# Second edge layer of a four-layer graph network: two of four message tiles weighed on ScalarE, scores copied from PSUM

## The chip, the cores and the metric

The kernel runs on one core of a Trainium2 chip. The metric is the device time of one launch in microseconds (us). It is a median of several runs; the kernel before has three. The profile is one execution of the same program. Its span runs from the first to the last recorded instruction.

## The reference

Four graph layers run one after the other over 50,000 nodes of 128 features and 25,000 edges, sorted by destination. Each adds its result to `x`. The change touches the second layer's edge pass:

```
h = max(layernorm(x), 0)
msgs = edge_weight[:, None] * h[src]
agg = segment_sum(msgs, dst)
x = x + agg @ W.T + b
```

The third layer is a graph attention layer. It needs, for every edge's destination, eight scores, and these are eight linear functions of the row `max(layernorm(x), 0)` after the second layer:

```
h = max(layernorm(x), 0)
(h @ W, a_src = h.att_src, a_dst = h.att_dst) -> 128 + 4 + 4 columns
```

## The kernel before, in words

All arithmetic is float32. The edges lie in 200 tiles of 125 edges, with one more row for what a segment carries over (126 rows, `RW`). Four tiles are a group (`GT` = 4), so that there are 50 groups (`NGE`). Each layer is a phase of its own, and the phases follow one another. The change lies in `phase_second`. Five engines run programs of their own there, tied by semaphores, as a software pipeline over steps `t`; at step `t` a group `g = t - k` is at stage `k`. One step therefore holds pieces of nine groups. On VectorE, ScalarE and SyncE the steps 12 to 43 stand in a loop of four steps a turn, the others are written out; TensorE's are all written out.

What is done for one group, with the line numbers of the profile:

- GpSimd issues four indirect DMAs (L526), which gather the 126 source rows of each tile into `second_xs`, four buffers. It may start on a group once ScalarE has finished the rows of the group four before (semaphore `rows`) and VectorE has copied its indices (L1240).
- VectorE subtracts a vector from `second_xs` (L1254), takes the statistics of each row (L1263, then L1294), and one step later 1/std and the bias (L1267, L1269). ScalarE takes the square root (L1324) between these.
- ScalarE normalises and applies Relu to each tile (L1314, `second_m<-second_xs`): four passes a group, each with a pointer for scale and one for bias.
- VectorE multiplies all four tiles `second_m` by the edge weights `k_wcol` in one instruction of 126x512 (L1258).
- TensorE turns the four tiles into `second_ps_agg` (L1365). VectorE runs a masked scan over them (L1306), which is the segment sum, into `second_at`. TensorE multiplies this by the layer's weights into `second_ps_y` (L1386), and VectorE adds it to the group's own rows `second_xp` (L1274). SyncE loads these rows (L1197) and stores them (L1216); it also loads the scan's mask (L1203).
- The statistics of the new rows are taken (L1284), ScalarE normalises them (L1314, `second_hr<-second_xp`), TensorE turns them (L1379), ScalarE copies the result to SBUF (L1348, `second_ht`), and TensorE makes `second_ps_g` of it, 136 columns a tile (L1395).
- ScalarE copies `second_ps_g` to SBUF as `second_g` (L1331) and signals `g_out`. SyncE stores `second_g` (L1210). VectorE copies the last eight columns of each tile from `second_g` to `l_SA` (L1290), with a pause on `g_out` before it, and signals `scores`, on which L1331 waits before it overwrites the buffer four groups later.

The order inside a step is written by hand, and the engines' queues are served in order. On VectorE it is L1240 (the indices of a later group), L1254, L1258, L1263 four times, L1267, L1269, L1274, two small copies (L1279, L1280), L1284 four times, L1290, L1294 eight times, L1306. On ScalarE it is L1324, L1331, four passes L1314 for `second_hr`, two for `second_m`, L1348, and the two other passes for `second_m`. On TensorE it is L1365, L1379, L1386, L1395. The statistics are awaited through the helper `gate`, which waits and then adds one to a semaphore that nobody reads:

```
def gate(kp, eng, sem, value):
    eng.wait_ge(sem, value)
    eng.sem_inc(kp.s_gate, 1)
```

## Time and profile before

| what | value |
|---|---|
| time, median of 3 runs | 3122.09 us |
| lowest and highest | 3106.39 and 3128.04 us |
| span of the profiled execution | 2606.6 us |
| second layer's edge pass, first gather to last score copy | 767.0 to 1092.1 us |
| VectorE (DVE) busy over the span | 78% |
| TensorE (PE) busy over the span | 73% |
| ScalarE (ACT) busy over the span | 66% |
| GpSimd (POOL) busy over the span | 50% |

The launch takes 515.5 us more than the span (3122.09 - 2606.6). The profiled execution has no separate time of its own beside its span here, so the two are set side by side: what lies around the span is taken as the same before and after. Shares over the whole span are a mean over the phases of four layers that have different limits; for a change in one phase the rows of that phase are to be read.

### The profile page before, as it was taken

How to read it: one execution, taken by the hardware profiler on the slowest of the kernel's cores; microseconds unless marked ns; L12 is line 12 of the kernel's file. 1: busy time of each engine (PE TensorE's matmuls, PEld its weight loads, DVE VectorE, ACT ScalarE, POOL GpSimd, SP SyncE). 2: the span in 40 equal slices, each digit the busy share in tenths (PEclk: the TensorE clock that was granted, in tenths of full speed). 3: DMA queues.
4: the chain of work that ended last, by engine and by line, in shares of the span. 5: the costliest groups of instructions: out<-in, count | busy, mean ns of one | idle time of the engine just before them, and what ended most of it. 6: DMA issues, size and time to landing. Idle time of an engine off the chain costs nothing. (4 is left out here: it accounts for less than half of the span.)

```text
span 2606.6 us, 48448 instructions
## 1 busy us (share of the span) xinstructions
PE 1899.9 (73%) x9715; PEld 1275.5 (49%) x9715; DVE 2027.9 (78%) x8016; ACT 1725.7 (66%) x4230; POOL 1311.4 (50%) x1309
## 2 busy tenths in 40 slices
PE   2445668888855666578884899566663999999996
PEld 1134445555534555468883444233332555555553
DVE  6855579999968999688885888588885777777773
ACT  3655679999965777589991444699994444444441
POOL 6755656666637666277760000000002677777773
PEclk9878889999986888889996999799997999999998
DMA  7989986666645777556662443699996544445540
GB/s 134 220 147 183 153 203 193 198 195 195 194 130 159 222 223 224 176 165 198 201 181 72 128 129 86 185 305 308 305 308 215 128 100 107 106 113 114 115 106 21
DMA packets 376244, 446.18 MB, mean 171 GB/s; under 512 B 103667, under 2 KB 225338, under 8 KB 376082
## 3 DMA queue, kind: packets, MB, share of 16 engines
q1 hardware_dynamic: 309970, 368.09, 50.8%
q0 software_dynamic: 59840, 74.08, 12.3%
q10 hardware_dynamic: 6272, 2.06, 0.5%
q8 instruction: 77, 1.26, 0.2%
q14 instruction: 85, 0.70, 0.1%
HBM read 288.86 MB, written 185.03 MB: 182 GB/s over the span
## 5 line engine op out<-in xcount | busy, mean ns | idle before, releaser
L2380 POOL DMA_INDIRECT mlp_bx<-t_X,k_bslot x2 | 2.0, 1012 | 611.7 <-POOLq L2647 611.4
L526 POOL DMA_INDIRECT second_xs<-t_XX,second_irs x200 | 205.4, 1027 | 115.8 <-issue 49.3
L2398 POOL DMA_INDIRECT out_dram<-mlp_ou,mlp_iro x200 | 212.6, 1063 | 83.2 <-issue 71.3
L2391 POOL DMA_INDIRECT mlp_xs<-t_X,mlp_irs x200 | 213.8, 1069 | 80.7 <-issue 55.7
L526 POOL DMA_INDIRECT project_xs<-t_XX,project_irs x200 | 199.6, 998 | 62.9 <-issue 58.3
L526 POOL DMA_INDIRECT a_xd<-in_x_dram,a_ird x152 | 152.6, 1004 | 129.1 <-DVE first_xo L968 84.9
L2439 DVE TENSOR_TENSOR_SCAN mlp_ms<-mlp_fm,mlp_ms,mlp_mm 128x500 f32<-128x500 f32 x98 | 123.4, 1260 | 120.2 <-ACT mlp_mm L2515 112.9
L2515 ACT ACTIVATE mlp_mm<-mlp_ps_m,mlp_bn 128x500 f32<-128x500 f32 x100 | 67.7, 677 | 187.1 <-PE mlp_ps_m L2575 187.1
L2265 PE MATMUL x_ps_o<-x_ht,x_wd 128*128 128x512 f32 (+1 forms) x198 | 117.1, 675 | 97.2 <-DVE x_ht L2165 81.1
L2575 PE MATMUL mlp_ps_m<-mlp_e,mlp_wn 128*128 128x504 f32 x400 | 185.3, 586 | 0.0
L2562 PE MATMUL mlp_ps_e<-mlp_h,mlp_we 128*128 128x504 f32 x400 | 179.5, 592 | 2.9 <-DVE mlp_h L2448 1.5
L2207 ACT ACTIVATE x_z<-x_x,x_nbm,l_mr 128x128 f32<-128x128 f32 x391 | 160.4, 488 | 14.2 <-DVE x_wd L2140 14.2
L1015 ACT ACTIVATE first_h<-first_x,first_nb,first_rs 128x128 f32<-128x128 f32 x391 | 159.9, 480 | 0.7 <-DVE first_nb L914 0.7
L526 POOL DMA_INDIRECT a_xs<-t_XR,a_irs x136 | 138.9, 1021 | 41.4 <-issue 41.4
L1623 ACT ACTIVATE project_h<-project_x,project_nb,project_rm 128x128 f32<-128x128 f32 x391 | 157.0, 515 | 0.0
L2508 ACT ACTIVATE mlp_e<-mlp_ps_e,mlp_be 128x504 f32<-128x504 f32 x100 | 68.1, 681 | 112.3 <-PE mlp_ps_e L2562 112.2
L876 DVE BATCH_NORM_STATS2 first_st<-first_x 128x6 f32<-128x128 f32 x391 | 81.1, 277 | 69.4 <-DMA first_x<-in_x_dram 69.4
L1942 ACT ACTIVATE attend_m<-attend_ps_o 1x132 f32<-1x132 f32 x199 | 53.6, 269 | 123.2 <-PE attend_ps_o L1986 119.9
L1314 ACT ACTIVATE second_hr<-second_xp,second_bi,second_rs 126x128 f32<-126x128 f32 x200 | 82.3, 482 | 74.9 <-DVE second_bi L1269 74.9
L2575 PEld LDWEIGHTS mlp_ps_m<-mlp_e,mlp_wn 128*128 128x128 f32 x400 | 76.0, 190 | 93.0 <-issue 93.0
L1638 PE MATMUL project_ps_gram<-project_h 128*128 128x129 f32 (+1 forms) x782 | 115.8, 295 | 6.4 <-ACT project_h L1623 6.2
L1112 PEld LDWEIGHTS first_ps_carry<-first_m,k_S 126*126 126x126 f32 x400 | 67.1, 198 | 102.1 <-issue 101.9
(411 smaller groups left out, 6343.3 us busy)
## 6 DMA issues: line engine op xcount, KB each, us to landing
first_x<-in_x_dram SPq DMA_DIRECT2D x97, 256.0 KB, 4.3
t_XX<-first_x SPq DMA_DIRECT2D x97, 256.0 KB, 2.7
project_x<-t_XX SPq DMA_DIRECT2D x97, 256.0 KB, 3.3
x_x<-t_XX SPq DMA_DIRECT2D x97, 256.0 KB, 4.3
t_X<-x_x SPq DMA_DIRECT2D x97, 256.0 KB, 3.7
out_dram<-x_ou SPq DMA_DIRECT2D x97, 256.0 KB, 4.7
t_XR<-in_x_dram SPq DMA_DIRECT2D x23, 1000.0 KB, 13.4
t_G<-second_g SPq DMA_DIRECT2D x50, 267.8 KB
```

The lines of the kernel that those rows point to most:

```text
L526: pool.indirect_dma_start(dst[:, q, lo:hi], None, table, bass.IndirectOffsetOnAxis(ap=idx[:, q:q + 1], axis=0)).then_inc(s_rows, 16)
L1015: ins = act.activation(Hh[2 * r + h][0:p, q, :], X[2 * u + h][0:p, q, :], ACT.Relu, bias=nb[r][0:p, c:c + 1], scale=rs[r][0:p, c:c + 1])
L1314: ins = act.activation(dst[:, q, :], x[:, q, :], ACT.Relu, bias=bi[k][:, w * GT + q:w * GT + q + 1], scale=rs[k][:, w * GT + q:w * GT + q ...
L1623: ins = act.activation(Hm[w][0:p, q, 0:128], X[2 * k + h][0:p, q, :], ACT.Relu, bias=nb[k][0:p, c:c + 1], scale=rm[k][0:p, c:c + 1])
L1638: ins = pe.matmul(psN[:, 0:129], Hm[w][0:p, q, 0:128], Hm[w][0:p, q, :], start=first, stop=final)
L2207: ins = act.activation(Z[s % 2][0:p, q, :], X2[s][0:p, q, :], ACT.Relu, bias=nbm[0:p, c], scale=kp.mr2[0:p, c, 1])
L2265: pe.matmul(featps(psO[s % 2], g), wd[:, :], feat(HTb[s % 2], g), start=True, stop=True).then_inc(s_o, 1)
L2391: pool.indirect_dma_start(Xs[u][:, q, :], None, T["X3"], bass.IndirectOffsetOnAxis(ap=irs[u][:, q:q + 1], axis=0)).then_inc(s_rows[u], 16)
L2398: pool.indirect_dma_start(out, bass.IndirectOffsetOnAxis(ap=iro[s][:, q:q + 1], axis=0), OU[s][:, q, :], None, bounds_check=N - 1, oob_is_ ...
L2439: dve.tensor_tensor_scan(Ms[r][:, h, 1:1 + E4], fm[f][:, :], Mb[r][:, h, :], init, ALU.mult, ALU.add).then_inc(s_ms, 1)
L2562: ins = pe.matmul(psE[h][:, 0:W4], we[:, w, h * 128:(h + 1) * 128], Hb[u][:, w, :], start=(w == 0), stop=(w == 1))
L2575: ins = pe.matmul(psM[h][:, 0:W4], wn1[:, w, h * 128:(h + 1) * 128], x, start=(w == 0), stop=(w == 2))
```

## The change

In the second layer's edge pass:

- VectorE weighs only tiles 2 and 3 of each group (126x256 in place of 126x512).
- ScalarE weighs tiles 0 and 1, in place, in two passes of 126x128 with function Copy and the edge weight as scale pointer. They stand at the end of its step, after all rows of `second_m`, behind a gate on a new semaphore `rows_by_scalar`, and signal `messages_by_scalar`.
- TensorE's first turn waits for both weighings.
- VectorE's copy to `l_SA` is gone. ScalarE makes it instead, directly from `second_ps_g`, right after L1331, and `g_out` is signalled by that second copy. The semaphore `scores` is gone with its two waits.

```
+WA = 2
...
             g2, s2 = t - 2, (u - 2) % 4
             if there(g2, NGE):
                 dve.wait_ge(s_h, g2 + 1)
-                dve.tensor_tensor(M[s2][:, :, :], M[s2][:, :, :],
-                                  kp.wcol[:, bass.ds(g2 * GT, GT)].unsqueeze(2).to_broadcast([RW, GT, 128]), ALU.mult).then_inc(s_m, 1)
+                dve.tensor_tensor(M[s2][:, WA:GT, :], M[s2][:, WA:GT, :],
+                                  kp.wcol[:, bass.ds(g2 * GT + WA, GT - WA)].unsqueeze(2).to_broadcast([RW, GT - WA, 128]), ALU.mult).then_inc(s_m, 1)
...
-            g8, s8 = t - 8, u
-            if there(g8, NGE):
-                dve.wait_ge(s_ge, g8 + 1)
-                dve.tensor_copy(kp.SA[:, bass.ds(g8 * GT, GT), :], G[s8][:, :, 128:GW]).then_inc(s_sa, 1)
...
+            if w == 0 and q == WA - 1:
+                ins.then_inc(s_h0, 1)
             if q == GT - 1:
                 ins.then_inc((s_h, s_hr)[w], 1)
...
-                    act.wait_ge(s_sa, g8 - 3)
-                act.activation(G[s8][:, :, :].rearrange("p (b q) w -> p b (q w)", b=2),
-                               psG[0:RW, :].rearrange("p (b w) -> p b w", b=2)[:, :, 0:2 * GW], ACT.Copy).then_inc(s_ge, 1)
+                out = psG[0:RW, :].rearrange("p (b w) -> p b w", b=2)[:, :, 0:2 * GW]
+                act.activation(G[s8][:, :, :].rearrange("p (b q) w -> p b (q w)", b=2), out, ACT.Copy)
+                act.activation(kp.SA[:, bass.ds(g8 * GT, GT), :].rearrange("p (b q) c -> p b q c", b=2),
+                               out.rearrange("p b (q w) -> p b q w", q=2)[:, :, :, 128:GW], ACT.Copy).then_inc(s_ge, 1)
...
+            if there(g1, NGE):
+                gate(kp, act, s_h0, g1 + 1)
+                for q in range(WA):
+                    ins = act.activation(M[s1][:, q, :], M[s1][:, q, :], ACT.Copy, scale=kp.wcol[:, bass.ds(g1 * GT + q, 1)])
+                ins.then_inc(s_m0, 1)
...
-                pe.wait_ge(s_m, g + 1)
+                pe.wait_ge(s_m0, g + 1)
+                gate(kp, pe, s_m, g + 1)
```

ScalarE's queue in the second layer's edge pass, one step just ahead of the loop, before (`second_m` are the messages, `second_ht` the turned rows, `second_g` the product's copy, `second_hr` the group's own rows):

```order
L1314 ACTIVATE second_m<-second_xs,second_bi,second_rs 126x128 [waits second_turned_messages]
L1314 ACTIVATE second_m<-second_xs,second_bi,second_rs 126x128
L1348 ACTIVATE second_ht<-second_ps_turn 128x504 [waits second_g,second_turned]
L1314 ACTIVATE second_m<-second_xs,second_bi,second_rs 126x128 x2
L1324 ACTIVATE second_sd<-second_mv,k_eps 126x8 [waits second_meanvar]
L1331 ACTIVATE second_g<-second_ps_g 126x544 [waits second_g]
L1314 ACTIVATE second_hr<-second_xp,second_bi,second_rs 126x128 [waits second_turned,second_bias]
```

The same engine and step in the change:

```order
L1311 ACTIVATE second_m<-second_xs,second_bi,second_rs 126x128 [waits second_turned_messages]
L1311 ACTIVATE second_m<-second_xs,second_bi,second_rs 126x128
L1348 ACTIVATE second_ht<-second_ps_turn 128x504 [waits second_g,second_turned]
L1311 ACTIVATE second_m<-second_xs,second_bi,second_rs 126x128 x2
L1356 ACTIVATE second_m<-second_m,k_wcol 126x128 [waits second_rows_by_scalar]
L1356 ACTIVATE second_m<-second_m,k_wcol 126x128
L1323 ACTIVATE second_sd<-second_mv,k_eps 126x8 [waits second_meanvar]
L1330 ACTIVATE second_g<-second_ps_g 126x544 [waits second_g]
L1331 ACTIVATE l_SA<-second_ps_g 126x32
L1311 ACTIVATE second_hr<-second_xp,second_bi,second_rs 126x128 [waits second_turned,second_bias]
```

Two passes L1356 now stand between the messages' rows and the square root, and one copy (L1331 of the change) between the copy of `second_ps_g` and the rows `second_hr`. The rows themselves (L1314 before, L1311 now) and L1348 keep their order.

VectorE's queue in the same pass, from the statistics of the new rows to those of the gathered rows, before:

```order
L1284 BN_STATS second_st<-second_xp 126x6 [waits second_x2]
L1284 BN_STATS second_st<-second_xp 126x6 x3
L1290 COPY l_SA<-second_g 126x32 [waits second_g_out]
L1294 BN_AGGR second_mv<-second_st 126x2 [waits second_stats]
L1294 BN_AGGR second_mv<-second_st 126x2 x7
L1306 SCALAR_TENSOR_TENSOR second_at<-second_fr,second_at,second_ps_agg 128x504 [waits second_mask_loaded2,second_summed,second_product,second_turned_messages]
L1240 COPY second_irs<-k_idx 126x4 [waits k_rows_gathered1]
L1254 TENSOR_TENSOR second_xs<-second_xs,k_b 126x512 [waits k_rows_gathered2]
L1258 TENSOR_TENSOR second_m<-second_m,k_wcol 126x512 [waits second_rows]
L1263 BN_STATS second_st<-second_xs 126x6 [waits second_x1]
```

And in the change:

```order
L1285 BN_STATS second_st<-second_xp 126x6 [waits second_x2]
L1285 BN_STATS second_st<-second_xp 126x6 x3
L1291 BN_AGGR second_mv<-second_st 126x2 [waits second_stats]
L1291 BN_AGGR second_mv<-second_st 126x2 x7
L1303 SCALAR_TENSOR_TENSOR second_at<-second_fr,second_at,second_ps_agg 128x504 [waits second_mask_loaded2,second_summed,second_product,second_turned_messages]
L1241 COPY second_irs<-k_idx 126x4 [waits k_rows_gathered1]
L1255 TENSOR_TENSOR second_xs<-second_xs,k_b 126x512 [waits k_rows_gathered2]
L1259 TENSOR_TENSOR second_m<-second_m,k_wcol 126x256 [waits second_rows]
L1264 BN_STATS second_st<-second_xs 126x6 [waits second_x1]
```

The score copy, which stood between the statistics and what waits for them (`second_stats`), is gone, and the weighing, which stands between the subtraction and what waits for it (`second_x1`), is half as wide. The scan stands in this list under another name than in the profile (TENSOR_TENSOR_SCAN).

## Rows read from the trace of the kernel before

**Rows 1.** Busy us: PE, PEld, DVE, ACT, POOL; then clock, DMA share, GB/s

```profile
826.00:1061.00 235.00, 147.40 (x961) 133.79 (x960) 229.56 (x1038) 173.92 (x440) 159.31 (x157) 0.87 0.76 223
```

**Rows 2.** Groups of instructions, 826 to 1061 us: xcount, busy us, mean ns, idle before

```profile
L1314 ACT ACTIVATE second_hr<-second_xp,second_bi,second_rs 126x128 f32<-126x128 f32 x160 | 65.9, 482 | 61.1 <-DVE second_bi L1269 61.1
...
L1386 PE MATMUL second_ps_y<-k_w1t,second_at 128*126 128x128 f32 x320 | 55.5, 328 | 1.0 <-DVE second_at L1306 0.3
...
L1258 DVE TENSOR_TENSOR second_m<-second_m,k_wcol 126x512 f32<-126x512 f32 x40 | 27.3, 684 | 0.0
```

**Rows 3.** Timeline, start us and us: VectorE's subtraction of groups 9 and 49

```profile
826.23 0.69 DVE L1254 TENSOR_TENSOR second_xs<-second_xs,k_b 126x512 f32<-126x512 f32 x1 [0.42 <-DMA second_xs<-t_XX,second_irs]
...
1060.91 0.67 DVE L1254 TENSOR_TENSOR second_xs<-second_xs,k_b 126x512 f32<-126x512 f32 x1
```

**Rows 4.** Groups of instructions over the whole span, VectorE, width 256

```profile
L1920 DVE TENSOR_TENSOR attend_sm<-k_S 126x256 f32 x36 | 15.0, 416 | 0.0
```

**Rows 5.** Timeline of VectorE, without the score copy (805 us) and with it (823 us)

```profile
805.17 0.86 DVE L1284 BATCH_NORM_STATS2 second_st<-second_xp 126x6 f32<-126x128 f32 x4
806.18 0.65 DVE L1294 BATCH_NORM_AGGREGATE second_mv<-second_st 126x2 f32<-126x6 f32 x8
...
822.81 0.86 DVE L1284 BATCH_NORM_STATS2 second_st<-second_xp 126x6 f32<-126x128 f32 x4
823.59 0.16 DVE L1290 COPY l_SA<-second_g 126x32 f32<-126x32 f32 x1
823.82 0.64 DVE L1294 BATCH_NORM_AGGREGATE second_mv<-second_st 126x2 f32<-126x6 f32 x8
```

**Rows 6.** Timeline, 898 to 911 us: two steps of the new rows, one product late

```profile
898.93 0.68 DVE L1274 TENSOR_TENSOR second_xp<-second_xp,second_ps_y 126x512 f32<-126x512 f32 x1
...
904.74 0.68 DVE L1274 TENSOR_TENSOR second_xp<-second_xp,second_ps_y 126x512 f32<-126x512 f32 x1
...
904.86 1.65 ACT L1314 ACTIVATE second_hr<-second_xp,second_bi,second_rs 126x128 f32<-126x128 f32 x4 [1.46 <-DVE second_bi L1269]
...
907.07 1.23 DVE L1306 TENSOR_TENSOR_SCAN second_at<-second_fr,second_at,second_ps_agg 128x504 f32<-128x504 f32 x1
...
907.90 1.07 PE L1379 MATMUL second_ps_turn<-k_ident,second_hr 126*128 126x126 f32 x4 [2.75 <-ACT second_ht L1348]
...
908.87 0.68 DVE L1258 TENSOR_TENSOR second_m<-second_m,k_wcol 126x512 f32<-126x512 f32 x1
...
910.71 0.69 DVE L1274 TENSOR_TENSOR second_xp<-second_xp,second_ps_y 126x512 f32<-126x512 f32 x1
```

**Rows 7.** Busy us while TensorE made a product in time and a late one

```profile
896.82:897.93 1.11, 1.11 (x10) 1.11 (x11) 1.11 (x3) 0.59 (x2) 0.34 (x1) 1.00 0.67 229
908.76:910.67 1.91, 1.91 (x11) 1.91 (x10) 1.84 (x8) 0.46 (x1) 1.04 (x1) 0.51 0.76 257
```

**Rows 8.** Timeline of ScalarE and TensorE, 896 to 899 us

```profile
896.62 0.29 ACT L1324 ACTIVATE second_sd<-second_mv,k_eps 126x8 f32<-126x8 f32 x1
...
896.81 0.60 ACT L1331 ACTIVATE second_g<-second_ps_g 126x544 f32<-126x544 f32 x1
...
897.77 1.09 PE L1395 MATMUL second_ps_g<-k_wg,second_ht 128*126 128x136 f32 x8
...
898.70 0.59 PE L1365 MATMUL second_ps_agg<-k_ident,second_m 126*128 126x126 f32 x4
```

**Rows 9.** Timeline of ScalarE and GpSimd, 907 to 916 us

```profile
907.66 0.86 ACT L1314 ACTIVATE second_m<-second_xs,second_bi,second_rs 126x128 f32<-126x128 f32 x2
...
909.38 1.04 POOL L526 DMA_INDIRECT second_xs<-t_XX,second_irs  x1 [0.88 <-ACT second_m L1314]
...
915.25 1.14 POOL L526 DMA_INDIRECT second_xs<-t_XX,second_irs  x1 [0.30 <-issue]
```

**Rows 10.** Timeline of VectorE past the last gather, 1067 us

```profile
1066.99 0.69 DVE L1258 TENSOR_TENSOR second_m<-second_m,k_wcol 126x512 f32<-126x512 f32 x1 [0.21 <-ACT second_m L1314]
```

**Rows 11.** Groups over the whole span, ScalarE, the narrowest copy out of PSUM

```profile
L994 ACT ACTIVATE first_ht<-first_ps_t 128x80 f32<-128x80 f32 x1 | 0.2, 236 | 0.0
```

More of the change, by code:

```diff
@@ L1176, in phase_second @@
     s_fr, s_a, s_at, s_y = m.ring("mask_loaded", 4), sem("turned_messages"), sem("summed"), sem("product")
-    s_x2, s_hr, s_t2, s_h2, s_g, s_ge, s_sa = (sem("x2"), sem("own_rows"), sem("turned"), sem("turned_out"),
-        sem("g"), sem("g_out"), sem("scores"))
+    s_x2, s_hr, s_t2, s_h2, s_g, s_ge = sem("x2"), sem("own_rows"), sem("turned"), sem("turned_out"), sem("g"), sem("g_out")
+    s_h0, s_m0 = sem("rows_by_scalar"), sem("messages_by_scalar")
     s_s2, s_sg = m.ring("x2_stored", 4), m.ring("g_stored", 4)
```

## The prediction

> **What bounds the kernel now.** I read the busy times of the second layer's pass by stretch first, because the shares over the whole launch mix the phases of four layers. From 826 to 1061 us VectorE is busy 229.56 of 235.00 us, 98%; ScalarE 74%, TensorE 63%, GpSimd 68% [rows 1]. Second, the groups of instructions of that stretch, last column: ScalarE was idle 61.1 us ahead of `second_hr`, all of it until VectorE's bias (L1269), which is 1.53 us in each of 40 steps. TensorE waits for ScalarE too, 2.75 us ahead of L1379 at 907.90 until `second_ht` [rows 6]. So VectorE sets the step and the others wait. Third, the timeline: VectorE's subtraction of group 9 starts at 826.23 and that of group 49 at 1060.91 [rows 3]: 234.7 us for 40 steps, 5.87 each. The row of group 9 also says that it waited for its gather; before that group the gathers set the pace, and a faster VectorE gains nothing there. The gain can only lie in these 40 steps.
>
> Within them one thing besides VectorE shows. The additions L1274 start at 898.93, 904.74 and 910.71: one step of 5.81 and one of 5.97 [rows 6]. Ahead of the last, TensorE's product L1386 ran from 908.76 to 910.67 and took 1.91 us at a granted clock of 0.51; the one before took 1.11 at 1.00 [rows 7]. The addition started 0.04 after the late product. How many products are late: L1386 is busy 55.5 us for 40 groups [rows 2]; at 1.11 each it would be 44.4; the rest, 11.1, over 0.80 a late one, is some 14. I take 13, as a few are late by half. Each adds 0.16 us (5.97 - 5.81).
>
> **The change part by part.**
>
> *The weighing on VectorE.* L1258 takes 684 ns at 126x512 [rows 2]. The same operation at 126x256 takes 416 ns in the attention phase [rows 4]. That is 0.268 us less a step. The weighing stands between the subtraction and the statistics that wait for it, and still covers that wait: such a wait ends 0.15 behind the instruction that it is for (1.01 - 0.86 [rows 5]), and the half weighing lasts 0.42. 40 steps give 10.7 us.
>
> *The score copy on VectorE.* L1290 takes 0.16 and stands between L1284 and L1294. But L1294 waits for the statistics to be written. With the copy, L1284 to L1294 is 823.82 - 822.81 = 1.01 us; in a step before the copies begin it is 806.18 - 805.17 = 1.01 as well [rows 5]. The wait hides the copy whole. Bounds: nothing, and 0.16 a step (6.4 us in all) if the wait were not there. I take nothing, since both rows are this very place.
>
> *The late products.* The product's end hangs on ScalarE: from the start of `second_hr` at 904.86 to the product's end at 910.67 is 5.81 us [rows 6, 7], by way of `second_ht` and L1379, and the new passes come behind these, so this stays 5.81. VectorE's own path from 904.86 to L1274 is 5.85 less the 0.16 of waiting, 5.69, and would be 5.42 with the shorter weighing. So if the clock still drops in 13 steps, each of these stays at 5.97 and gains nothing. If it does not, each gains 0.27 + 0.16. What decides is when TensorE idles. Now its longest idle stretch is 2.75 us ahead of L1379, and L1379 then ran at half the clock (1.07 us for four turns) [rows 6]. In the change `second_g` and then the score copy come later: 3.57 us for `second_hr`, L1348 and `second_m` (908.52, the end of the last row at L1314 [rows 9], less 904.86 and the 0.09 by which passes overlap), two weighings of 0.39, the square root 0.19, L1331 0.60, the copy 0.15, is about 5.3 (the last three from rows 8 and 11). So L1395 and L1365 (1.09 and 0.59 [rows 8]) run from 5.4 to 7.1, and L1379 follows at 5.54 (the step of 5.81 less 0.27) + 3.04 (907.90 - 904.86) = 8.6. The idle stretch shrinks to some 1.5 us; a shorter one opens ahead of L1395. I take the clock to hold in these steps. In the Trainium skill, "TensorE: Matmul & The Clock Gate" (Why this matters for your kernels) advises against long idle stretches of TensorE between bursts, because the clock falls back to 1.2 GHz; the drop behind 2.75 us of idleness agrees, and by that rule the late products go.
>
> *ScalarE's new work.* Four passes of L1314 take 1.65 us [rows 6], so one costs 0.39 behind another (482 ns alone [rows 2]). The weighing has one pointer operand fewer; I take 0.39; bounds 0.15 (the 236 ns copy of 128x80 without pointers, less 0.09 of overlap [rows 11]) and 0.48. The score copy is narrower than that copy of 128x80; I take 0.15, bounds nothing and 0.24. In all 0.93 a step, bounds 0.30 and 1.20. ScalarE has 1.53 idle, less the 0.27 by which the step shrinks: 1.26. It fits, and at the upper bound it just does. The Trainium skill, "ScalarE: Activation LUTs" (Rules for kernel authors), speaks against the move: it wants multiplications on VectorE. The rows agree on the price, 0.78 here against 0.268 there for two tiles, but the dearer engine is the idle one. Its section "What ACT_TABLE_LOAD costs" prices a pass by its pointers, 186 ns + 0.833 ns an element + 93 ns for each; by it a weighing is 386 ns alone and 0.29 behind another, and ScalarE's sum would be 0.73.
>
> *The new waits.* The square root comes 0.78 later on ScalarE. VectorE's L1267 needs it behind L1258, which starts at 908.87 - 904.86 = 4.01 [rows 6], behind half a weighing (0.34 until the next starts) and four statistics (0.78), at 5.13; it ends at 3.57 + 0.78 + 0.29 = 4.64. Slack 0.5. The scan waits for L1365, done at 7.1; the scan stands at 907.07 - 904.86 = 2.21 of the next step, 7.75. Slack 0.6; behind it would queue all of VectorE. `second_m` for VectorE is ready at 908.52, wanted at 908.87 [rows 6, 9], unchanged. The store of `second_g` waits for `g_out`, some 0.9 later (0.78 + 0.15), and behind it on SyncE stand the loads of the next state and mask and the state's store; all are wanted about two steps later. GpSimd waits for `rows`, which fires as before, ahead of the weighing: in 5.2 to 5.4 us (four issues of 1.0 to 1.04 with 0.30 between [rows 9]) it is through with a group, so it keeps up with 5.54. The gathers' landing is wanted up to 0.54 us sooner, which the depth of four buffers covers but for a step or two.
>
> *The last steps.* Past the last gather VectorE waits for ScalarE: L1258 by 0.21 [rows 10]. There the two weighings lie on the path in two steps: at most 0.78 - 0.27 = 0.51 each, nothing if ScalarE idles as long there; I take 0.25; in the last three groups the copy at 0.15 is ahead of `g_out`, +0.45. Together +1.0.
>
> **The sum.** 27 steps at 0.268 = 7.2; 13 at 0.43 = 5.6; the end gives 1.0 back: -11.8. The profiled span goes from 2606.6 to 2594.8. With the 515.5 us around it, as it stands to the median: 3122.1 - 11.8 = 3110.3 us. Three runs of before lie 21.7 us apart, so that a measurement tells about 1% (31 us) from no change; this gain is 0.4%.
>
> **The rivals.**
>
> *The clock still drops (0.22).* For it: TensorE has no more work than before, and in most steps the clock holds although the wait ahead of L1379 is there in all of them, so that wait alone does not decide. Against: the idle stretch nearly halves. Then 27 x 0.268 - 1.0 = 6.2, 3115.9 us.
>
> *The score copy counts too (0.08).* For it: 0.16 us of busy VectorE go in each step. Against: rows 5. 11.8 + 6.4 = 18.2, 3103.9 us.
>
> *GpSimd or the gathers take over (0.12).* For it: GpSimd waited 0.88 ahead of 909.38 on ScalarE although the rows had ended at 908.52, and its group then lasted to 915.25, 5.87 us, as long as a step [rows 9]; if each restart cost that, its pace would stay 5.8 and the gain would be what the buffers' lead allows, some 3 us: 3119 us. Against: the issue at 915.25 came 0.30 behind the one before, since its release, due a step behind 908.52, had come while it was still issuing. A late GpSimd pays no restart.
>
> *ScalarE becomes the bound, and it gets slower (0.04).* The mechanism: two passes and a copy in one in-order queue ahead of the square root and `second_hr`. It decides once they cost more than the 1.53 idle. At 1.9 us (each in-place pass also waiting for what it reads) the step would be 0.37 longer: 40 x 0.37 + 2 = +17, 3139 us. Against: the price bound is 1.20.
>
> *The change does not do what it says (0.07).* VectorE's instruction may not halve, for instance because its time is not by width. Then all that stays is the end: 3123. Against: rows 4.
>
> **How the numbers follow.** My forecast has 0.47. The cases reach from 3103.9 to 3123 without the slower one; the unknown costs move each by 3 us. The runs' own spread puts about 10 us around a median. That gives 3095 to 3126 for 8 in 10. Faster by over 1% would need 31 us, nearly three times the forecast: 0.04. Slower by over 1% asks of the slower rival twice its price: 0.03. Within 1%: 0.93.
>
> **What would show it.** Right: the weighing at 416 ns; L1284 to L1294 still at 1.01 us; steps of 5.54; 40 steps in some 222 us; the clock in the stretch above 0.87 and no addition behind a late product; ScalarE idle 0.3 to 0.6 a step until the bias. Wrong: VectorE idle on the square root or on L1365, GpSimd without any wait while VectorE waits for gathers, or a step still at 5.8.

## The result, and the profile after

| | median | lowest to highest |
|---|---|---|
| before, 12 runs | 3105.42 us | 3085.75 to 3128.04 |
| the change, 12 runs beside them | 3127.76 us | 3101.53 to 3146.33 |

The ratio is 1.007, 95% interval 1.0046 to 1.0095: slower by 0.7%, some 22 us, where 12 us less were forecast. The profiled execution of the change has a span of 3130.6 us and a time of its own of 3132.14, so only 1.5 us lie around the span. In the 19 profiled executions that have a time of their own it is 1.5 to 1.6 us. The 515.5 us that the prediction put around the span of before therefore lay inside the span of its ordinary executions: the execution traced before the prediction was unlike its timed runs. A second trace of the same kernel, taken later, has a span of 3076.2 us (time 3077.74) and is the one to compare with. (Each trace is one execution, and the chips differ: in the batch of the second trace the median of before is 3055.6 us.)

The second trace of before is 470 us longer than the first. Where they lie is told by phase. Three stretches of the first trace of before: the projection, the attention pass, the last layer (columns as in [rows 1]):

```profile
1095.00:1384.00 289.00, 229.34 (x1788) 219.35 (x1788) 229.35 (x1642) 261.59 (x691) 201.80 (x206) 0.89 0.61 179
1422.00:1633.00 211.00, 189.62 (x804) 101.62 (x804) 169.89 (x551) 81.10 (x250) 0.00 (x0) 0.97 0.43 120
1998.00:2583.00 585.00, 558.00 (x2200) 320.37 (x2200) 429.19 (x1500) 251.37 (x500) 421.72 (x398) 0.98 0.46 106
```

The same three in the second trace of before:

```profile
1323.00:1728.00 405.00, 279.55 (x1788) 262.03 (x1788) 240.32 (x1642) 264.08 (x691) 202.87 (x206) 0.74 0.44 128
1765.00:1977.00 212.00, 189.42 (x804) 101.49 (x804) 170.21 (x553) 81.51 (x251) 0.00 (x0) 0.97 0.43 119
2341.00:3053.00 712.00, 601.28 (x2200) 336.20 (x2200) 430.67 (x1500) 245.97 (x500) 409.83 (x398) 0.92 0.38 87
```

The phase without GpSimd work (fifth busy column 0.00) lasts as long; those in which GpSimd gathers are 116 and 127 us longer. GpSimd's own busy time is about the same in them (201.80 and 202.87, 421.72 and 409.83 us), so it is not its instructions that are longer.

The second layer, over the same 40 steps as [rows 3] (the subtraction of group 9 to that of group 49), second trace of before:

```profile
1012.26:1290.12 277.86, 164.14 (x960) 147.85 (x960) 230.15 (x1039) 176.15 (x439) 163.76 (x156) 0.79 0.64 187
```

The change:

```profile
1035.80:1350.55 314.75, 173.29 (x963) 152.49 (x961) 216.80 (x999) 203.63 (x562) 156.73 (x157) 0.73 0.57 167
```

[Rows 1] had 98% of the stretch busy on VectorE. It is 83% in the ordinary execution of before and 69% in the change. VectorE's work did fall, 230.15 to 216.80 us, a third of a microsecond a step; its idle time grew from 48 to 98 us. What VectorE waits for, second trace of before:

```profile
DVE second_xp L1274 <- remote: 39.6, 12, 5.3
```

And in the change:

```profile
DVE second_xp L1275 <- remote: 88.2, 15, 8.7
POOL second_xs L527 <- DVE second_irs L1241: 82.8, 11, 9.3
```

"Remote" is a release that the profile ties to no instruction. The addition waits for two things, the rows that SyncE loads (L1197, L1198 in the change) and TensorE's product (L1386, L1392 in the change); which one it was is read below. [Rows 6] had no such wait. GpSimd then waits for VectorE (second row of the change) and starts late in its turn.

Groups of the change that answer to [rows 2] and [rows 4]:

```profile
L1392 PE MATMUL second_ps_y<-k_w1t,second_at 128*126 128x128 f32 x320 | 61.6, 353 | 85.4 <-DVE second_at L1303 58.7 <-issue 26.4
...
L1356 ACT ACTIVATE second_m<-second_m,k_wcol 126x128 f32<-126x128 f32 x81 | 27.6, 389 | 0.0
...
L1259 DVE TENSOR_TENSOR second_m<-second_m,k_wcol 126x256 f32<-126x256 f32 x40 | 16.7, 417 | 0.0
```

The half weighing takes 417 ns, as forecast. One such wait in the timeline, 1077 to 1097 us of the change (SPq is SyncE's queue):

```profile
1077.53 2.04 PE L1392 MATMUL second_ps_y<-k_w1t,second_at 128*126 128x128 f32 x8 [7.85 <-DVE second_at L1303]
...
1078.09 0.35 SPq L1211 DMA_DIRECT2D t_G<-second_g  x1
...
1078.85 0.34 SPq L1198 DMA_DIRECT2D second_xp<-t_XX  x1
...
1079.46 0.38 SPq L1204 DMA_DIRECT2D second_fr<-t_f  x1
...
1079.61 0.69 DVE L1275 TENSOR_TENSOR second_xp<-second_xp,second_ps_y 126x512 f32<-126x512 f32 x1 [0.15 <-PE second_ps_y L1392]
...
1080.36 0.86 DVE L1285 BATCH_NORM_STATS2 second_st<-second_xp 126x6 f32<-126x128 f32 x4
1080.53 0.36 SPq L1217 DMA_DIRECT2D t_XX<-second_xp  x1
...
1081.36 0.64 DVE L1291 BATCH_NORM_AGGREGATE second_mv<-second_st 126x2 f32<-126x6 f32 x8
...
1083.06 0.68 ACT L1356 ACTIVATE second_m<-second_m,k_wcol 126x128 f32<-126x128 f32 x2
...
1084.02 1.00 POOL L527 DMA_INDIRECT second_xs<-t_XX,second_irs  x1 [8.55 <-DVE second_irs L1241]
...
1084.34 0.18 ACT L1331 ACTIVATE l_SA<-second_ps_g 126x32 f32 x1
...
1085.14 0.68 DVE L1275 TENSOR_TENSOR second_xp<-second_xp,second_ps_y 126x512 f32<-126x512 f32 x1
...
1085.32 1.00 POOL L527 DMA_INDIRECT second_xs<-t_XX,second_irs  x1 [0.30 <-issue]
...
1086.08 0.71 SPq L1198 DMA_DIRECT2D second_xp<-t_XX  x1
...
1087.58 0.01 SPq L1204 DMA_DIRECT2D second_fr<-t_f  x1
...
1088.84 1.12 PE L1392 MATMUL second_ps_y<-k_w1t,second_at 128*126 128x128 f32 x8
...
1089.78 0.72 SPq L1217 DMA_DIRECT2D t_XX<-second_xp  x1
1089.79 1.00 POOL L527 DMA_INDIRECT second_xs<-t_XX,second_irs  x1 [0.86 <-issue]
...
1093.50 0.69 SPq L1211 DMA_DIRECT2D t_G<-second_g  x1
1093.68 1.00 POOL L527 DMA_INDIRECT second_xs<-t_XX,second_irs  x1 [0.30 <-issue]
...
1095.88 0.34 SPq L1198 DMA_DIRECT2D second_xp<-t_XX  x1
...
1096.67 0.69 DVE L1275 TENSOR_TENSOR second_xp<-second_xp,second_ps_y 126x512 f32<-126x512 f32 x1 [5.90 <-remote]
```

Read it from above. GpSimd has been waiting for VectorE, 8.55 us. Meanwhile SyncE issues its four transfers within 2.4 us, and the step from the addition at 1079.61 to that at 1085.14 is 5.53, the forecast step. At 1084.02 GpSimd starts, and issues eight gathers, two groups, until 1094.68. From 1085.32 SyncE's issues lie 1.5 to 3.7 us apart. The product is drawn as finished at 1089.96 (1088.84 + 1.12), and yet VectorE stands for 5.90 us, until 1096.67. That stall makes GpSimd wait again, and so on.

**What the addition waits for.** It is not the load. The addition at 1096.67 is that of group 12, and the load of its rows is the one at 1078.85, 17.8 us earlier; SyncE loads two steps ahead, and the load at 1095.88 is that of group 14. The next stall, of group 15, settles it. Its load was issued at 1101.97, and VectorE passed the wait for it (L1274 of the change) at 1113.5, before it stood still. That wait, and the timeline:

```profile
L1274 DVEq EVENT_SEMAPHORE  x1: 21/21/21, 1113.5 to 1113.5; - x1
```

```profile
1101.97 0.34 SPq L1198 DMA_DIRECT2D second_xp<-t_XX  x1
...
1111.91 1.92 PE L1392 MATMUL second_ps_y<-k_w1t,second_at 128*126 128x128 f32 x8
...
1121.45 0.69 DVE L1275 TENSOR_TENSOR second_xp<-second_xp,second_ps_y 126x512 f32<-126x512 f32 x1 [7.84 <-remote]
```

What is left is TensorE's product. The profile models the ends of matmuls; the semaphores are recorded by themselves. The semaphore `product`, which only TensorE's last matmul of a group raises, went up at 1121.43, 7.6 us behind the drawn end (1113.83), and the addition began 0.02 later. For group 12 it went up at 1096.54, 6.6 us behind the drawn end, and ScalarE's copy of `second_ps_g` too began just behind TensorE's signal for it (1100.28, drawn as due at 1091.59):

```profile
1100.30 0.62 ACT L1330 ACTIVATE second_g<-second_ps_g 126x544 f32<-126x544 f32 x1 [0.91 <-remote]
```

The same holds of every stall. Of the additions in the 40 steps of all traces, 192 stood for over 0.8 us, and each of them was then at its wait for `product`. In the second trace of before 61 of 131 recorded updates of TensorE's four semaphores come over 0.5 us behind the drawn end, in the change 76 of 145, up to 10 us; in the first trace none of 160. By phase, such late signals stand in all five phases in which GpSimd gathers (8, 158, 66, 116 and 122 of them in the second trace of before) and in neither of the two in which it does not. So VectorE waits for a late product, as the prediction had it in some steps, but by microseconds and not by 0.16.

**SyncE pauses in the same phases**, in the middle of plain instructions, where it waits for nothing. Its instructions for the mask in the second trace of before (counts; shortest/median/longest ns; first and last start):

```profile
L1203 SPq DMA_DIRECT2D second_fr<-t_f x40: 3/362/707, 1013.4 to 1286.3; - x40
L1203 SPq MOVE second_fr<-t_f x36: 3/16/703, 1035.3 to 1281.7; - x36
```

And in the first trace:

```profile
L1203 SPq DMA_DIRECT2D second_fr<-t_f x40: 362/378/1264, 827.6 to 1057.3; - x40
L1203 SPq MOVE second_fr<-t_f x36: 29/29/29, 846.3 to 1051.9; - x36
```

A register move that takes 29 ns took up to 703. I added all stops of SyncE of 0.3 us or more outside its waits on semaphores and outside its DMA instructions: 0.4 us in the 40 steps of the first trace, 72.3 in the second, 111.6 in a second trace of the change. Sorted by what GpSimd does (stops of over 0.45 us, DMA instructions included), second trace of before: 81 us of pauses in the 219 us in which GpSimd was issuing, 2 us in the 58 in which it was not. In the change: 117 in 212, and 10 in 102. So these pauses fall into the time in which GpSimd issues gathers. They are no wait of VectorE's: each of the 192 additions had had its load issued 9.8 us or more before it began to stand.

### The profile page after: what moved, and what is told of

It is laid out like the page before. It is cut to its first block and busy times, and to the rows that moved or that the text cites. A ratio compares the mean times of both kernels' runs of the same rounds, so it can differ in the third digit from the quotient of the medians.

```text
span 3130.6 us, 48609 instructions
## 1 busy us (share of the span) xinstructions
PE 2072.0 (66%) x9715; PEld 1388.0 (44%) x9715; DVE 2033.9 (65%) x7966; ACT 1767.6 (56%) x4380; POOL 1296.7 (41%) x1309
## 5 line engine op out<-in xcount | busy, mean ns | idle before, releaser
L2397 POOL DMA_INDIRECT mlp_xs<-t_X,mlp_irs x200 | 203.9, 1020 | 195.7 <-issue 130.8
L2404 POOL DMA_INDIRECT out_dram<-mlp_ou,mlp_iro x200 | 212.5, 1063 | 94.8 <-issue 93.9
L2568 PE MATMUL mlp_ps_e<-mlp_h,mlp_we 128*128 128x504 f32 x400 | 199.3, 646 | 23.1 <-ACT mlp_h L2548 10.8
L1113 PE MATMUL first_ps_carry<-first_m,k_S 126*126 126x128 f32 x400 | 99.8, 336 | 144.8 <-ACT first_m L987 108.1
L1113 PEld LDWEIGHTS first_ps_carry<-first_m,k_S 126*126 126x126 f32 x400 | 76.7, 224 | 235.7 <-issue 235.6
L2514 ACT ACTIVATE mlp_e<-mlp_ps_e,mlp_be 128x504 f32<-128x504 f32 x100 | 66.5, 678 | 202.3 <-DMA t_XD<-hist_d 127.3
L527 POOL DMA_INDIRECT a_xs<-t_XR,a_irs x136 | 138.0, 1014 | 77.3 <-ACT first_m L1030 38.7
L1644 PE MATMUL project_ps_gram<-project_h 128*128 128x129 f32 (+1 forms) x782 | 140.3, 325 | 33.8 <-issue 27.4
L2521 ACT ACTIVATE mlp_mm<-mlp_ps_m,mlp_bn 128x500 f32<-128x500 f32 x100 | 66.1, 677 | 148.2 <-PE mlp_ps_m L2581 71.4
L1644 PEld LDWEIGHTS project_ps_gram<-project_h 128*128 128x128 f32 (+1 forms) x782 | 126.2, 238 | 42.5 <-issue 32.7
L1392 PE MATMUL second_ps_y<-k_w1t,second_at 128*126 128x128 f32 x400 | 77.4, 355 | 98.4 <-DVE second_at L1303 67.7
L987 ACT ACTIVATE first_m<-first_ps_carry 1x128 f32<-1x128 f32 x199 | 50.7, 255 | 155.0 <-remote 146.5
```

Of the source, the lines that this page charges most:

```text
L527: pool.indirect_dma_start(dst[:, q, lo:hi], None, table, bass.IndirectOffsetOnAxis(ap=idx[:, q:q + 1], axis=0)).then_inc(s_rows, 16)
L1113: pe.matmul(psC[0:RW, 128 * q:128 * (q + 1)], s0, M[r][:, q, :], start=True, stop=True).then_inc(e_co, 1)
L1644: ins = pe.matmul(psN[:, 0:129], Hm[w][0:p, q, 0:128], Hm[w][0:p, q, :], start=first, stop=final)
L2397: pool.indirect_dma_start(Xs[u][:, q, :], None, T["X3"], bass.IndirectOffsetOnAxis(ap=irs[u][:, q:q + 1], axis=0)).then_inc(s_rows[u], 16)
L2404: pool.indirect_dma_start(out, bass.IndirectOffsetOnAxis(ap=iro[s][:, q:q + 1], axis=0), OU[s][:, q, :], None, bounds_check=N - 1, oob_is_ ...
L2568: ins = pe.matmul(psE[h][:, 0:W4], we[:, w, h * 128:(h + 1) * 128], Hb[u][:, w, :], start=(w == 0), stop=(w == 1))
```

## The experiments

The kernels ran in five batches behind the first comparison, on chips that differ (median of before 3109 and 3112 in the batches f and j, 3056 to 3059 in b and e, g, h), so ratios to before in the same batch are compared. The columns behind the ratio come from one traced execution each, and only b0 is a trace of before among them; the traced execution of f1 was 19 us shorter than the median of its kernel, that of f3 9 us longer. "Steps" is the distance from one addition to the next, counted from the addition of group 9 to that of group 45; a stalled step is one over 6.5 us, and its stall the excess over 5.8. The shortest step is some 0.07 us below the usual unstalled one (5.74 and 5.81 in before).

| kernel | ratio, 95% interval | 40 steps, us | shortest step | stalled, sum us | pauses of SyncE, us |
|---|---|---|---|---|---|
| before, first trace | | 234.7 | 5.73 | 0 | 0.4 |
| b0 before again | 1.0031 (0.9993 to 1.007) | 277.9 | 5.74 | 13, 38.7 | 72.3 |
| e1 weighing only | 1.0041 (1.0001 to 1.0081) | 291.0 | 5.47 | 13, 53.8 | 89.6 |
| e2 score copy only | 1.0023 (0.9995 to 1.0052) | 277.4 | 5.74 | 12, 39.4 | 89.5 |
| e3 change, weighing later | 1.0065 (1.0032 to 1.0098) | 290.1 | 5.47 | 11, 51.8 | 93.9 |
| f0 the change again | 1.0096 (1.0064 to 1.0127) | 320.1 | 5.48 | 13, 80.0 | 111.6 |
| f1 before, half unweighed | 1.0041 (1.0013 to 1.0069) | 292.8 | 5.48 | 12, 53.2 | 105.7 |
| f2 before, ScalarE more | 1.0051 (1.0018 to 1.0084) | 302.5 | 5.73 | 12, 64.2 | 87.0 |
| f3 change, filler 256 | 0.9995 (0.997 to 1.002) | 292.1 | 5.81 | 12, 48.6 | 79.7 |
| g0 before, filler 256 | 0.9927 (0.989 to 0.9964) | 246.4 | 6.07 | 0 | 18.5 |
| g1 before, filler 512 | 0.9965 (0.9927 to 1.0002) | 257.0 | 6.34 | 7, 5.1 | 10.5 |
| g2 before, mask by ScalarE | 1.0014 (0.998 to 1.0048) | 276.7 | 5.73 | 12, 37.8 | 42.8 |
| g3 change, mask by ScalarE | 1.0072 (1.0036 to 1.0107) | 301.5 | 5.47 | 11, 64.3 | 66.5 |
| h0 before, no mask loads | 0.9993 (0.9954 to 1.0032) | 269.5 | 5.73 | 11, 32.0 | 41.2 |
| h1 change, no mask loads | 1.0027 (0.9995 to 1.006) | 289.4 | 5.47 | 12, 51.7 | 53.2 |
| h2 change, filler 512 | 0.9897 (0.9861 to 0.9934) | 246.9 | 6.07 | 0 | 18.3 |
| h3 before, filler 64 | 0.9994 (0.9959 to 1.0029) | 271.8 | 5.87 | 9, 30.7 | 66.1 |
| j0 before, no gathers | 0.9797 (0.9734 to 0.986) | 234.7 | 5.73 | 0 | 0.4 |
| j1 change, no gathers | 0.9741 (0.968 to 0.9801) | 223.6 | 5.47 | 0 | 0.4 |

### The parts, and the order

b0 is before itself. e1 is the change without the score copy's move, e2 that move alone, e3 the change with ScalarE's two passes put behind the score copy, one step later:

```
+                gate(kp, act, s_h0, g2 + 1)
+                for q in range(WA):
+                    ins = act.activation(M[s2][:, q, :], M[s2][:, q, :], ACT.Copy, scale=kp.wcol[:, bass.ds(g2 * GT + q, 1)])
+                ins.then_inc(s_m0, 1)
```

> The kernel before, unchanged, for a second trace of it. The first trace of it has a span of 2606.6 us while its timed runs take 3105 us; the trace of the change has 3130.6. Both theories expect a ratio of 1.000 +- 0.003 and a span near 3105. Queue theory: the waits of VectorE for the load of the state (L1274, some 7 us every third step in the change) are in this trace too, and the second edge layer lasts some 360 to 385 us in place of the 325 of the first trace. Other theory (the waits come with the change): no such waits, the layer lasts 325 us and the 500 us are elsewhere.

> The change with the score copy put back on VectorE; ScalarE still weighs two tiles ahead of the square root. Queue theory (SyncE serves its queue in order behind the signal of second_g, and sets the layer's pace; what makes that signal later costs time): the signal is 0.68 us later instead of 0.86, so most of the loss stays, +13 to +20 us against the kernel before. Rival (the loss is the score copy's, which reads PSUM on the way to TensorE and SyncE): 0 or a gain of up to 10 us.

> The score copy alone moves to ScalarE; VectorE weighs all four tiles. Queue theory: the signal is only some 0.15 us later, +2 to +6 us against the kernel before. Rival (the loss is the score copy's): +15 to +25 us.

> The change with ScalarE's two weighings moved behind the copies out of PSUM, one step later, so that the square root and second_g come as early as in the kernel before (the signal only 0.15 us later). Queue theory: the loss goes, -5 to +6 us against the kernel before. Rival (the two passes cost wherever they stand, or the shorter VectorE step itself collides with the transfers): +15 to +25 us as in the change.

Measured: b0 has the stalls without the change, and its ratio of 1.0031 shows what two runs of one kernel can differ by. e2 leaves the 40 steps where they were (277.4 against 277.9) and the shortest step at 5.74, so the copy's move is worth nothing, as predicted. e1 has the shorter step and lasts 13 us longer. e3, in which the product leaves PSUM as early as before, is no better than e1 (290.1 and 291.0). The theory that SyncE only waits longer for `g_out` falls.

### Shorter VectorE step against more ScalarE work

f0 is the change. f1 is before with the half-width weighing and nothing in its place, so that two tiles of each group stay unweighed:

```
-                dve.tensor_tensor(M[s2][:, :, :], M[s2][:, :, :],
+                dve.tensor_tensor(M[s2][:, WA:GT, :], M[s2][:, WA:GT, :],
```

f2 is before with two ScalarE passes into a scratch tile that nobody reads, where the change has its weighing; f3 is the change with a product of 126x256 on VectorE into such a tile, right behind the weighing:

```
+                dve.tensor_tensor(scratch[:, :, :], kp.b1[0:RW, 0:2, :], kp.b1[0:RW, 0:2, :], ALU.mult)
```

> The change itself once more, beside the next three on one chip. Ratio to the kernel before 1.004 to 1.010, and 40 steps of the layer (L1255 of group 9 to that of group 49) in 288 to 315 us against 278 of the kernel before. Step theory (where VectorE asks sooner, SyncE, whose issues set the pace, falls behind sooner and its issues get slower, so the stalls of VectorE grow by more than its steps shrink) and pass theory (ScalarE's two more passes delay what SyncE waits for or slow the issues themselves) say the same of this run.

> The kernel before, with VectorE weighing tiles 2 and 3 alone; tiles 0 and 1 are not weighed by anyone, ScalarE has no new pass and TensorE no new wait. Its time shows the shorter VectorE step alone. Step theory: slower than the kernel before by 10 to 20 us, 40 steps in about 290 us, its unstalled steps 5.47 us. Pass theory: no slower, 0 to -10 us, 40 steps in 265 to 278 us.

> The kernel before with two passes of 126x128 more on ScalarE in the place where the change weighs, on a scratch tile that nobody waits for; VectorE weighs all four tiles. Pass theory: slower by 10 to 20 us, 40 steps in about 290 us. Step theory: within 4 us of the kernel before, 40 steps in 274 to 282 us.

> The change, with a multiplication of 126x256 on a scratch tile added on VectorE right behind its half weighing, so that its step is as long as before (two fixed costs instead of one: some 0.07 us longer) while ScalarE keeps its passes. Step theory: the loss goes, -3 to +6 us against the kernel before, 40 steps in 276 to 283 us. Pass theory: the loss stays, +13 to +25 us.

Measured: each half of the change alone is slower by its ratio, though by little more than the 0.3% between before and itself in b0. Taking work away from VectorE and giving it to nobody makes the launch 0.4% longer; more work on ScalarE alone 0.5%; the change is 1.0% longer. Giving VectorE useless work takes all of that back (f3), clear of the noise. The traces do not follow as well: f3 was expected at 276 to 283 us for the 40 steps and has 292.1, as much as f1, and f0 with 320.1 is over the 315 expected.

### A filler in before and in the change

g0, g1 and h3 add a scratch product of 126x256, 126x512 and 126x64 to before; h2 adds the 126x512 one to the change.

> The kernel before with a multiplication of 126x256 on a scratch tile added on VectorE behind its weighing: unstalled steps 0.34 us longer, nothing else. Stall theory (SyncE's instructions pause by some 0.7 us each while transfers crowd; a VectorE that asks sooner makes more of these pauses, one that asks later fewer): faster than or equal to the kernel before, -12 to 0 us. Rival (VectorE's step is simply added, as it would be were it the bound): +8 to +14 us.

> The same with 126x512: unstalled steps 0.6 us longer. Stall theory: -15 to +5 us, as the step of 6.4 us is still under the 6.95 that the layer takes on average. Rival: +20 to +26 us.

> The change with a scratch multiplication of 126x512 on VectorE behind its half weighing: unstalled steps of 5.47 + 0.60 = 6.07 us, the same as the kernel before with the filler of 126x256. If ScalarE's passes cost nothing of their own: ratio 0.990 to 0.997 and 40 steps in 244 to 250 us, as there. If they have a cost of their own (the run with two extra passes alone was 0.5% slower): ratio 0.997 to 1.003, 40 steps over 255 us.

> The kernel before with a scratch multiplication of 126x64 on VectorE: unstalled steps 0.12 us longer, 5.87 or so. It looks for the point at which the stalls set in: a sharp one between 5.8 and 6.1 gives either the full gain (ratio 0.990) or none (1.000); a gradual one gives a part, ratio 0.994 to 0.998 and 40 steps in 255 to 272 us, which I expect.

Busy times of the 40 steps of g0:

```profile
1009.04:1255.39 246.35, 154.25 (x963) 140.81 (x962) 241.93 (x1079) 174.34 (x441) 170.19 (x157) 0.84 0.72 213
```

And of h2:

```profile
1029.56:1276.49 246.93, 156.34 (x962) 137.58 (x961) 239.09 (x1039) 200.96 (x561) 169.72 (x157) 0.87 0.72 213
```

VectorE does 12 us more in g0 than in b0, is 98% busy again, and the stretch is 31.5 us shorter. The launch gains 22 us, where at most 12 were expected. No addition of g0 or h2 stands for over 0.8 us. h2 and g0 have the same shortest step, 6.07, by different ways, and last the same 40 steps: at this step ScalarE's passes and the score copy cost nothing that shows. h3, at 5.87, still stalls in 9 steps, and its ratio of 0.9994 misses the part of the gain that was expected (0.994 to 0.998); g1, at 6.34, gives some of the gain back as longer steps. (Its 7 steps over 6.5 are 5.1 us in all.) So in these executions the stalls end between a shortest step of 5.87 and one of 6.07 us. h2 is faster than both kernels, by 1.0% against before; its interval overlaps that of g0.

### SyncE's load

g2 and g3 are before and the change with the mask's load issued by ScalarE, so that SyncE has three transfers a step, not four. h0 and h1 issue the mask's load for the first four groups only; every later scan takes one of these four masks, so that the two leave out part of the layer's work.

```
-            if there(g, NGE):
-                if not before(g, 4):
-                    gate(kp, sp, s_at, g - 3)
+            if before(g, 4):
```

> The kernel before with the loads of the scan's mask issued by ScalarE in place of SyncE, which keeps three transfers a step. If SyncE's issues set the pace: the layer gets shorter, 40 steps in 240 to 265 us, the kernel faster by 12 to 40 us. If the transfers themselves are the limit (bandwidth, contention with the gathers), it is the same whoever issues them: within 4 us.

> The change, with the mask's loads issued by ScalarE. If SyncE set the pace and no longer does, the shorter VectorE step counts as the prediction had it: 5 to 12 us less than the same edit on the kernel before, against the 20 to 30 us more that the change costs without it. If the transfers are the limit, it stays 20 to 30 us over the other.

> The kernel before without the loads of the scan's mask from group 4 on: every scan takes one of the first four groups' masks. This leaves out 252 KB of the 1276 KB that a step transfers. Traffic theory (a step of 5.8 us asks more of the transfers than they give in an ordinary execution, and then they give less still; SyncE's pauses are how it shows): the stalls go without any filler, 40 steps in 232 to 240 us, kernel faster than the one before by 35 to 50 us. Rival (a step under 6 us stalls by the engines' timing, whatever the traffic): 40 steps in 265 to 278 us.

> The change without the loads of the scan's mask from group 4 on, as in the run before this. Traffic theory: with the traffic gone VectorE sets the pace, and the change is worth what the prediction gave it: 8 to 12 us faster than the same edit on the kernel before, 40 steps in 220 to 228 us. Rival: 15 to 30 us slower than that one.

Measured: a quarter of SyncE's issues moved away, or left out with 10 MB of the stretch's 52, and the stalls stay: 12 and 11 in before, 11 and 12 in the change. The pauses of SyncE do shrink, from 72.3 us in b0 to 42.8 and 41.2, while the stalls of before go from 38.7 to 37.8 and 32.0 only: one more sign that VectorE does not stand because of SyncE. The number of transfers or bytes on SyncE's queue makes neither.

### Without the gathers

j0 and j1 are before and the change in which GpSimd gathers for the first four groups and then only waits and signals; the rest of the layer works on stale rows.

```
+                if before(t, 4):
+                    gather_rows(pool, Xs[u], T["XX"][0:ROWS, :], irs[u], s_rows[u])
+                else:
+                    pool.sem_inc(s_now, 1)
```

> The kernel before; GpSimd gathers only for the first four groups of the second layer and afterwards only passes its two waits and signals (this leaves out the gathering of the other 46 groups, so the scan works on stale rows; VectorE, ScalarE, TensorE and SyncE do all their work). Theory A (the pauses of SyncE in this layer come with GpSimd's gathers): the 40 steps from the subtraction of group 9 to that of group 49 last 228 to 238 us (VectorE's own 5.75 to 5.87 a step), no step over 6.5 us, pauses of SyncE under 20 us of 40 steps, where the ordinary execution of before has 277.9 us, 13 stalled steps and 72.3 us. The launch is 40 to 60 us shorter, a ratio of 0.980 to 0.987. Theory B (the pauses have another source, such as SyncE's own transfers or the loop on SyncE): stalls as before, 265 us or more, ratio 0.995 to 1.0.

> The change with the same gathers left out. Theory A: what was predicted of the change appears, steps of 5.45 to 5.60, 218 to 226 us for the 40 steps, 8 to 12 us less than the run beside it, so a ratio 0.003 to 0.004 below its ratio. Rival (a step under 5.9 us stalls whatever GpSimd does): the change is again longer than the run beside it by 8 us or more, with stalled steps at the addition. Theory B: 290 us or more for the 40 steps.

The 40 steps of j0:

```profile
1021.73:1256.38 234.65, 147.31 (x963) 133.66 (x962) 229.15 (x1039) 174.29 (x441) 0.00 (x0) 0.87 0.59 179
```

And of j1:

```profile
1018.64:1242.20 223.56, 154.02 (x962) 133.14 (x961) 215.25 (x999) 200.88 (x561) 0.00 (x0) 0.88 0.61 188
```

j0 is [rows 1] again, to the tenth: 234.65 us against 234.68, clock 0.87. Its move for the mask takes 29 ns throughout:

```profile
L1205 SPq MOVE second_fr<-t_f x36: 29/29/29, 1042.0 to 1247.4; - x36
```

j1 is 11.1 us shorter than j0 over the 40 steps, where with the gathers the change lasts 37 us longer than b0 (in its first profile, on another chip). (The medians of j0 and j1 lie 22 us apart, from four runs each with intervals that overlap; where the rest of that comes from was not looked for.) Without the gathers all 160 recorded updates of TensorE's semaphores come on time in both, no addition stands for over 0.8 us, SyncE's pauses are down to 0.4 us, and the loss is gone. It is not the bytes as such: the gathers moved 10 MB of the stretch (187 GB/s over 277.86 us with them in b0 is 52 MB, 179 over 234.65 without them is 42), as much as the mask's loads, whose absence changed little in h0. Whether it is GpSimd's issuing or the kind of its transfers was not separated.

## Why the prediction was wrong

**The step that failed** is "VectorE sets the step and the others wait", and with it the price of a late product, 0.16 us in 13 steps, which the change was to remove. In an ordinary execution of before VectorE is busy for 83% of the 40 steps, and the addition waits for a late product 39.6 us in 12 waits, up to 5.3 each; in the change 88.2 us in 15, up to 8.7. The 0.268 us a step that the weighing gives did come, and went into longer waits: 314.8 us for the 40 steps against 277.9, where 12.8 less were forecast.

It failed because of the base of the sum: "With the 515.5 us around it, as it stands to the median". Time less span was put down as something outside the program that stays the same. It was 1.5 to 1.6 us in every later profile. The missing time was idle time inside the phases that gather, which the one trace did not have, and the change works in one of them. The sum came out right for executions like the traced one, as j0 and j1 are, and no timed run of before or the change was of that kind. (The 3122.1 that it starts from is a median of three; of twelve it is 3105.42, so the forecast of the difference was off by 34 us, more than the 17.5 between 3110.3 and 3127.76.)

**Point by point.** The weighing on VectorE at 416 ns: 417. Steps of 5.54: the shortest are 5.47, the one shown is 5.53. The score copy worth nothing: e2's shortest step of 5.74 is that of b0. L1284 to L1294 still at 1.01 us: 1081.36 - 1080.36 = 1.00 in the change's timeline. ScalarE's passes at 0.39 each and the copy at 0.15: two passes in 0.68 (1083.06), not 0.78, and a copy of 0.18 (1084.34). ScalarE idle 0.3 to 0.6 us a step until the bias: 22.7 us over 40 steps in j1, 0.57. "40 steps in some 222 us": 223.6 in j1, 314.8 in the change. The gain over the 40 steps, forecast at 12.8 (7.2 + 5.6): 11.1 between j0 and j1.

**The clock** did not hold as forecast. The late products are, by the prediction's own count (busy time over 44.4, by 0.80), 13 in j0 and 8 in j1:

```profile
L1397 PE MATMUL second_ps_y<-k_w1t,second_at 128*126 128x128 f32 x320 | 54.7, 325 | 1.3 <-DVE second_at L1317 0.5
```

```profile
L1403 PE MATMUL second_ps_y<-k_w1t,second_at 128*126 128x128 f32 x320 | 50.7, 308 | 0.8 <-DVE second_at L1314 0.6
```

The rule cited there, of "TensorE: Matmul & The Clock Gate" in the Trainium skill, names the right direction: with stalls of 6 to 9 us in the stretch the granted clock fell to 0.73, and a product drawn behind 7.85 us without matmuls took 2.04 us (1077.53), one in an even step 1.12 (1088.84). It did not follow that a shorter idle stretch keeps the clock: ahead of the turn of the new rows (L1379) TensorE was idle 88.8 us in j0 and 55.6 in j1, 2.2 and 1.4 a step, and the granted clock was 0.87 and 0.88.

**The rivals.** None named what happened. The nearest was "The clock still drops": it had the late product, but as late by 0.16 us, through the clock. At a granted clock of 0.50 the product took 2.04 us in place of 1.12 at 1.00, and the signals came 6 to 8 us late, so the clock does not explain them. What the prediction said of SyncE's transfers, that they "are wanted about two steps later", held: they are issued that early, and no addition waited for one, even where SyncE paused.

**The cause, as far as shown.** VectorE stands because TensorE's signal of the product comes late: each of the 192 stalled additions was at that wait. The gathers are a condition: without them the signals are on time and the change gains 11.1 us (j0, j1). The pace is another: at a shortest step of 6.07 us or more there is next to nothing of it, at 5.87 and below there is (h2 and g0; h3), and more in f1, e1 and f0, with 5.47 and 5.48, than in b0. (That the stalls grow evenly with the pace is not shown: f3, at 5.81, has more of them than b0.) The change shortens the step and adds ScalarE work, and each of the two alone was slower. That the stall keeps itself going (VectorE late, so GpSimd late, so two or three groups of gathers in a row, so TensorE late, so VectorE late) is read from the timeline and was not tried alone; neither was a slower GpSimd beside an unchanged VectorE. Open stay: what holds TensorE up, and SyncE with it, while gathers are issued; why the first trace of before was free of it at a shortest step of 5.73 us, with the gathers; and why more ScalarE work costs at 5.73 (f2) and nothing at 6.07. The other phases that gather were not changed.

## What to carry to other kernels

Set time beside span before anything else: where they differ by more than a few microseconds, the trace may be of another kind of execution than the timed ones, and a sum made on it need not hold for them; the phases in which the difference lies should be named first. A pipeline in which an engine is 98% busy can be one that only just keeps off a stall elsewhere; there a shorter step can cost, and a scratch instruction on the bounding engine is a cheap test (here it gained 0.7 to 1.0%). Where a wait is put down to "remote", look at every semaphore that the instruction waits for, and at which group each transfer belongs to: here the load beside the stall was that of another group, and the matmuls' drawn ends hid that the product was late.

## What the runs showed of the hardware

TensorE's signals came up to 10 us behind the ends that the profile draws for its matmuls, in every phase in which GpSimd gathered and in no other (0 late ones in the two phases without gathers, 8 to 158 in the five with them, second trace of before), and none did with the gathers of the layer left out. SyncE's plain register moves, 29 ns each, took up to 703 ns in the same execution, and two of its DMA instructions lay 1.5 us apart (1086.08 and 1087.58 in the timeline above) where the same two lay 0.6 apart a step before (1078.85 and 1079.46); with the gathers left out this vanished. The first trace of before had neither, with all its gathers. The Trainium skill, "DMA: Bandwidth & Descriptors" (Issuing engines are not separate DMA queues), calls the sequencer's time to start a transfer usually small beside the transfer; the load at 1078.85 agrees, with 0.34 us for the issue and the last update of its semaphore at 1082.63, 3.8 us behind it. The pauses depend on the pace: 18 us of them in 246 at a shortest step of 6.07, 72 in 278 at 5.74 and 112 in 320 at 5.48, with the same instructions on SyncE and GpSimd. A launch of more work (g0, with a scratch product of 126x256 in each of 50 steps) ended 0.7% sooner.
